# An attention loop on one core: shift by four reductions, token queries on two other engines, f32 products first in a group's last pair, all pair sums kept

## The chip, the cores and the metric

The kernel runs on one core of one Trainium2 chip. A core has TensorE (PE, matrix products, with weight loads shown as PEld), VectorE (DVE), ScalarE (ACT), GpSimd (POOL) and SyncE (SP), which issues most of the DMAs. The metric is the device time of the whole program in microseconds (us), lower is better. The kernel before takes 576.8 us (median of 3 runs, 575.64 to 578.02).

## The reference

Three layers stand behind each other: cross attention of 512 tokens (4 batches of 128, width 512) to 2048 context rows for each batch, a gated scan, and a mixture of 8 experts with two shared ones. The change touches the attention alone:

```
x = x + xattn(layernorm(x), ctx, ctx)
  q = x.reshape(B, T, 16, 32) * 32**-0.25          # 16 heads of 32
  k = ctx.reshape(B, S, 16, 32) * 32**-0.25; v = ctx.reshape(B, S, 16, 32)
  w = softmax(einsum('bthd,bshd->bhts', q, k))
  out = einsum('bhts,bshd->bthd', w, v).reshape(B, T, W) @ w_proj.T + b_proj
```

## The kernel before

The attention is cut into G = 16 groups: one batch and four heads (128 columns) each. A group needs, for each of its 4 heads, scores of 128 tokens against 2048 keys. Keys and queries are split into a high and a low float16 part, and three products (high x high, low x high, high x low) are stacked along the contraction, so KS = 96 rows give scores close to float32.

A group j passes through these steps, spread over the two groups before it:

- `split_keys(j, ...)`: ScalarE casts the float32 keys `kt` to `kh` (2 casts of 1024 elements to a partition), GpSimd subtracts to get `kl` (4 subtractions of 512, L587). SyncE's DMAs stack `kh`, `kl`, `kh` into `kstk`.
- `token_queries(j)` (L684, VectorE): two casts of the normed tokens into `xs` (L689, L690: the high part, twice) and one subtraction (L692: the low part). `queries(j)` (PE) transposes them and `take_queries` (ScalarE) copies them to `q1`.
- 16 times `max_scores(j, k)` (PE, L974: 512 keys of one head, into one of two PSUM banks) and `take_max` (VectorE, L697: the maximum along the 512). Product k waits until maximum k-2 has been taken, so PE and VectorE go in step with at most two between them.
- `shift(j)` (VectorE): the negated maximum of the four parts of a head (L701), its float16 high part (L704) and its low part (L706) go into two more columns of `xs`. `shifted(j)` (PE, L981) transposes the whole and `take_shifted` (ScalarE, L451) copies it to `q2`. So the maximum is subtracted within the score product.
- 8 times `scores(n)` (PE, L994: 2 tiles of 128 keys x 4 heads), `exponent(n)` (ScalarE, L462, 1024 elements), `values(n)` (PE, L1009, float32 products that weight `v`) and a denominator. The exponentials stand in a ring `pt` of 4. For 6 of the 8 numbers n of a group GpSimd adds the two tiles (`pair_sum`, L606) and PE multiplies the sum by ones (`denominators`, L1018: 4 float32 products); for the two in `PLAIN = (3, 7)` PE multiplies both tiles (`direct_denominators`, L1026: 8 products).
- `invert(i)` (L714) and `divide(i)` (L718) on VectorE, once all denominators of group i are there.

The order on each engine is written out by hand and is strict. PE's loop goes over pairs p = 0 to 3 of group i. In a pair it does, in this order, some maximum products of the next group (p = 3: of the one after), the two score products for numbers 8i+2p+2 and 8i+2p+3 with maximum products between them, the denominators of the pair before, `values` of 8i+2p and 8i+2p+1, and the direct denominators. In p = 1 `queries(i+2)` is put in; after p = 2 comes `shifted(i+1)`, and the scores of p = 3 are the first ones that need its `q2`. `MAXIMA` says how many maximum products stand in p = 0 to 3: 4, 4, 3, 5. ScalarE does in each pair the two exponentials, then `take_queries` (p = 1), a cast of the keys of group i+3 (p = 0, 1) or `take_shifted` (p = 2). GpSimd does the pair sums in order and, after numbers 3 and 5, two key subtractions each. VectorE takes the maxima of the pair, then `invert` and `divide` of the group before (p = 0), `shift(i+1)` (p = 2), `token_queries(i+3)` (p = 3). The last two groups have less beside them: no keys are split from group 13 on, and group 15 has no maxima of a next group.

SyncE loads keys three to four groups ahead and values one, and issues the constants and six weight tiles of the last layer during groups 13 and 14.

Of the kernel before, what the change touches and what calls it, by code (L numbers as in the profile page):

```python
# [83 lines left out]
def build_program(nc, t, out):  # L84
# [66 lines left out]
    mx = temp("mx", [P, HG, HG], F32)  # L151
    negm = temp("negm", [P, HG], F32)
    rden = temp("rden", [P, P], F32)
# [62 lines left out]
    win_done = sem("win_scaled")  # L216
    xs_step = sem("xs_step")
    qT_ready = sem("queries_transposed")
# [10 lines left out]
    den_done = sem("den_done")  # L229
    direct_done = sem("direct_denominators_done")  # L230
    o_rd = sem("o_reciprocal")
# [64 lines left out]

    PLAIN = (3, 7)
    SUMS = [hs for hs in range(HS) if hs not in PLAIN]
    NS, ND = len(SUMS), len(PLAIN)
    MAXIMA = (range(5, 9), range(9, 13), range(13, MB), range(0, 5))  # L300

    def sums(n):

        return NS * (n // HS) + len([hs for hs in SUMS if hs < n % HS])

    def plain(n):

        return n - sums(n)

    def is_plain(n):  # L310
        return n % HS in PLAIN

    def block_of(k):
        h, k = divmod(k, 2 * HG)
        return k // 2, 2 * h + k % 2

    def maxima_in(i, p):
# [106 lines left out]
    def _(act):  # L424
# [22 lines left out]
        def take_shifted(j):  # L447
            act.wait_ge(sh_ready, j + 1)
            if j >= 2:
                act.wait_ge(st_done, HS * (j - 1))  # L450
            act.activation(q2[:, j % 2, :, :], half_bank(6 + j % 2)[0:KM, 512:1024]  # L451
                           .rearrange("k (a t) -> k a t", a=HG), ACT.Copy).then_inc(q2_done, 1)

        def exponent(n):
            act.wait_ge(st_done, n + 1)
            if n >= 4:
                act.wait_ge(pv_done, n - 3)
                if is_plain(n - 4):
                    act.wait_ge(direct_done, plain(n - 3))
                else:  # L460
                    act.wait_ge(add_done, sums(n - 3))
# [6 lines left out]
        act.wait_ge(eps_set, 2)  # L468
        root(ln1_var, 1, 0, 1)
        for h in range(2):  # L470
            split_keys(1, h)
# [6 lines left out]
        exponent(0)  # L478
        exponent(1)
        for i in range(G):  # L480
# [102 lines left out]
    def _(pool):  # L583
# [10 lines left out]
        pool.memset(eps[:, 0:1], EPS).then_inc(eps_set, 1)  # L594
        pool.memset(eps[:, 1:2], EPS * 1e-8).then_inc(eps_set, 1)
        for a in range(2, HG):
            split_keys(0, a)
        for j in range(1, 3):
            for a in range(HG):
                split_keys(j, a)  # L600

        def pair_sum(n):
            pool.wait_ge(exp_done, n + 1)
            if sums(n) >= 4:
                pool.wait_ge(den_done, sums(n) - 3)
            pool.tensor_tensor(ps2[:, sums(n) % 4, :, :], pt[:, n % 4, 0, :, :], pt[:, n % 4, 1, :, :], ALU.add)\  # L606
                .then_inc(add_done, 1)
# [63 lines left out]
    def _(dve):  # L671
# [11 lines left out]

        def token_queries(j):  # L684
            q = xn[:, :, :].rearrange("p b (c n) -> p (b c) n", c=C)[:, j, :].rearrange("p (a d) -> p a d", a=HG)
            z = xs[:, j % 2, :, :]
            if j >= 2:
                dve.wait_ge(sh_ready, j - 1)
            dve.tensor_copy(z[:, :, 0:HD], q).then_inc(xs_step, 1)  # L689
            dve.tensor_copy(z[:, :, HD:2 * HD], q).then_inc(xs_step, 1)  # L690
            dve.wait_ge(xs_step, 3 * j + 1)
            dve.tensor_tensor(z[:, :, 2 * HD:KS], q, z[:, :, 0:HD], ALU.subtract).then_inc(xs_step, 1)  # L692

        def take_max(j, k):
# [4 lines left out]
        def shift(j):  # L699
            dve.wait_ge(m_taken, MB * (j + 1))  # L700
            dve.tensor_reduce(negm[:, :], mx[:, :, :], AX.X, ALU.max, negate=True).then_inc(mx_step, 1)  # L701
            dve.wait_ge(mx_step, 3 * j + 1)
            z = xs[:, j % 2, :, :]
            dve.tensor_copy(z[:, :, KS:KS + 1], negm[:, :].unsqueeze(2)).then_inc(mx_step, 1)  # L704
            dve.wait_ge(mx_step, 3 * j + 2)
            dve.tensor_tensor(z[:, :, KS + 1:KM], negm[:, :].unsqueeze(2), z[:, :, KS:KS + 1], ALU.subtract)\  # L706
                .then_inc(mx_step, 1)

        def invert(i):
            dve.wait_ge(den_done, NS * (i + 1))  # L710
            dve.wait_ge(direct_done, ND * (i + 1))
# [25 lines left out]
        dve.wait_ge(xn_done, 1)  # L737
        token_queries(0)
        token_queries(1)
        dve.wait_ge(x_in, 16)  # L740
# [4 lines left out]
        for j, k in maxima_in(-1, 3):  # L745
            take_max(j, k)
        token_queries(2)
        dve.wait_ge(roots, 2)
# [9 lines left out]
        for i in range(G):  # L758
            if i == G - 1:
                scale_win()  # L760
            for p in range(HS // 2):
# [5 lines left out]
                if p == 2 and i + 1 < G:  # L767
                    shift(i + 1)
                if p == 3 and i + 3 < G:
                    token_queries(i + 3)  # L770
        invert(G - 1)
# [184 lines left out]
    def _(pe):  # L956
        def queries(j):
            pe.wait_ge(xs_step, 3 * j + 3)
            if j >= 3:
# [17 lines left out]
        def shifted(j):  # L977
            pe.wait_ge(mx_step, 3 * j + 3)
# [35 lines left out]
        def denominators(n):  # L1014
            i, hs = divmod(n, HS)
            pe.wait_ge(add_done, sums(n) + 1)
            for a in range(HG):
                mm = pe.matmul(bank[a * HD:(a + 1) * HD, 6 + i % 2, P:2 * P], ones[:, :], ps2[:, sums(n) % 4, a, :],  # L1018
                               start=False, stop=(hs == SUMS[-1]), skip_group_check=True)
            mm.then_inc(den_done, 1)  # L1020

        def direct_denominators(n):
            i = n // HS
            for j in range(2):
                for a in range(HG):
                    mm = pe.matmul(bank[a * HD:(a + 1) * HD, 6 + i % 2, P:2 * P], ones[:, :], pt[:, n % 4, j, a, :],  # L1026
                                   start=False, stop=False, skip_group_check=True)
            mm.then_inc(direct_done, 1)

# [6 lines left out]
        shifted(0)  # L1036
        for i in range(-1, G):
            for p in range(HS // 2):
                if i < 0 and p < 3:
                    continue  # L1040
                tenants = maxima_in(i, p)
                for j, k in tenants[0:2]:
                    max_scores(j, k)
                for a, n in enumerate(scores_in(i, p)):
                    scores(n)
                    if p == 1 and a == 0 and i + 2 < G:
                        queries(i + 2)
                    for j, k in tenants[2 + a:3 + a]:
                        max_scores(j, k)
                for j, k in tenants[4:]:  # L1050
                    max_scores(j, k)
                if i < 0:
                    continue
                done = [HS * i + 2 * p, HS * i + 2 * p + 1]
                for n in (done[0] - 2, done[1] - 2):
                    if n >= 0 and not is_plain(n):
                        denominators(n)
                for n in done:
                    values(n)
                for n in done:  # L1060
                    if is_plain(n):
                        direct_denominators(n)
                if p == 2 and i + 1 < G:
                    shifted(i + 1)
        denominators(HS * (G - 1) + SUMS[-1])


# [241 lines left out]
```

## Time and profile before

| | us |
|---|---|
| median of 3 runs | 576.8 (575.64 to 578.02) |
| the profiled execution | 577.4 |
| its span, first to last instruction | 575.6 |
| PE busy | 484.5 (84%) |
| VectorE busy | 445.1 (77%) |
| ScalarE busy | 327.4 (57%) |
| GpSimd busy | 254.1 (44%) |

The attention fills the span's first 320 us or so. The profile is one execution; the busy shares are means over stages with different limits, so the stage of the attention is to be read by itself. The mean granted TensorE clock is 0.966 of full speed.

### The profile page before, as it was taken

How to read it: one execution, taken by the hardware profiler on the slowest of the kernel's cores; microseconds unless marked ns; L12 is line 12 of the kernel's file. 1: busy time of each engine (PE TensorE's matmuls, PEld its weight loads, DVE VectorE, ACT ScalarE, POOL GpSimd, SP SyncE). 2: the span in 40 equal slices, each digit the busy share in tenths (PEclk: the TensorE clock that was granted, in tenths of full speed). 3: DMA queues.
4: the chain of work that ended last, by engine and by line, in shares of the span. 5: the costliest groups of instructions: out<-in, count | busy, mean ns of one | idle time of the engine just before them, and what ended most of it. 6: DMA issues, size and time to landing. Idle time of an engine off the chain costs nothing.

```text
span 575.6 us, 16203 instructions
## 1 busy us (share of the span) xinstructions
PE 484.5 (84%) x6987; PEld 339.7 (59%) x6987; DVE 445.1 (77%) x635; ACT 327.4 (57%) x344; POOL 254.1 (44%) x230
## 2 busy tenths in 40 slices
PE   0468988889888898888998984879799999999993
PEld 0025666657666666665666561734488888887641
DVE  3576888888888888888872489888359999999416
ACT  3245655667556666557556253555349888888310
POOL 2356656777567676576546550456101110110050
PEclk9999989999899999899999996798899999999998
DMA  8696877677877778656599513239748999998143
GB/s 257 124 297 204 241 231 200 170 211 221 240 208 187 186 216 254 203 116 180 144 324 403 219 62 146 74 128 412 279 151 304 421 418 417 415 419 352 38 130 109
DMA packets 48252, 133.98 MB, mean 233 GB/s; under 512 B 6450, under 2 KB 31282, under 8 KB 37426
## 3 DMA queue, kind: packets, MB, share of 16 engines
q1 hardware_dynamic: 44500, 120.88, 64.7%
q0 software_dynamic: 3680, 12.06, 5.8%
q8 instruction: 55, 0.90, 0.6%
q14 instruction: 17, 0.14, 0.1%
HBM read 96.74 MB, written 11.01 MB: 187 GB/s over the span
## 4 chain that ended last, share of the span: by engine, by line
DVE 46%; PE 31%; issue 8%; DMA 8%; POOL 4%; ACT 2%; SPq 1%; DVEq 0%; ACTq 0%
DVE mx L697 17%; DVE ws L776 8%; PE bank L974 4%; PE bank L1009 4%; DMA kt<-in_keysT 4%; PE bank L994 3%; POOL xs_rows L651 3%; DVE xs L706 3%; PE bank L1018 3%; PE bank L1074 2%; DVE xs L690 2%; DVE rden L714 2%; DMA wst<-in_ffw 2%; DVE xs L704 2%; PE bank L1026 2%
## 5 line engine op out<-in xcount | busy, mean ns | idle before, releaser
L697 DVE TENSOR_REDUCE mx<-bank 128x1 f32<-128x512 f32 x256 | 163.3, 684 | 50.3 <-PE bank L974 49.2
L462 ACT ACTIVATE pt<-bank 128x1024 f32<-128x1024 f32 x128 | 128.2, 1023 | 81.7 <-PE bank L994 80.1
L606 POOL TENSOR_TENSOR ps<-pt 128x512 f32<-128x512 f32 x96 | 121.2, 1275 | 85.0 <-ACT pt L462 83.9
L776 DVE SCALAR_TENSOR_TENSOR ws<-wst,ws 128x2048 f16<-128x2048 f32 x51 | 116.5, 2301 | 2.3 <-ACT ws L501 2.1
L974 PE MATMUL bank<-kstk,q 96*128 96x512 f16 x256 | 95.0, 413 | 21.3 <-DVE mx L697 9.2
L501 ACT ACTIVATE ws<-wst 128x2048 f16<-128x2048 f32 x48 | 90.5, 1904 | 9.8 <-PE bank L1214 6.6
L587 POOL TENSOR_TENSOR kl<-kt,kh 128x512 f16<-128x512 f32 x62 | 70.5, 1160 | 40.3 <-ACT kh L432 40.3
L994 PEld LDWEIGHTS bank<-q,kstk 98*128 98x128 f16 x1024 | 69.0, 100 | 32.5 <-ACT q L451 12.9
L994 PE MATMUL bank<-q,kstk 98*128 98x128 f16 x1024 | 81.2, 225 | 5.5 <-ACT q L451 4.9
L1146 PE MATMUL bank<-xt,ws 128*128 128x128 f16 x480 | 81.2, 219 | 0.1
L1148 PE MATMUL bank<-xt,ws 128*128 128x128 f16 x480 | 81.2, 219 | 0.0
L1147 PE MATMUL bank<-xt,ws 128*128 128x128 f16 x480 | 81.2, 219 | 0.0
L1009 PE MATMUL bank<-pt,v 128*32 128x128 f32 x2048 | 69.6, 277 | 1.5 <-issue 1.5
L644 POOL DMA_DIRECT2D ys_rows<-xn x15 | 8.2, 543 | 120.3 <-ACT xn L568 120.3
L1009 PEld LDWEIGHTS bank<-pt,v 128*32 128x32 f32 x2048 | 58.8, 112 | 2.6 <-issue 2.3
L974 PEld LDWEIGHTS bank<-kstk,q 96*128 96x128 f16 x256 | 21.2, 100 | 50.4 <-DVE mx L697 33.1
L1146 PEld LDWEIGHTS bank<-xt,ws 128*128 128x128 f16 x480 | 47.0, 98 | 0.6 <-DVE hf L914 0.6
L432 ACT ACTIVATE kh<-kt 128x1024 f16<-128x1024 f32 x32 | 33.3, 1049 | 24.5 <-DMA kt<-in_keysT 24.5
L1148 PEld LDWEIGHTS bank<-xt,ws 128*128 128x128 f16 x480 | 47.0, 98 | 0.0
L1147 PEld LDWEIGHTS bank<-xt,ws 128*128 128x128 f16 x480 | 47.0, 98 | 0.0
L914 DVE SCALAR_TENSOR_TENSOR hf<-bank,win 128x512 f32<-128x512 f32 x23 | 15.8, 685 | 29.7 <-PE bank L1133 23.4
L1018 PE MATMUL bank<-ps,ones 128*32 128x128 f32 x768 | 35.7, 289 | 0.0
(163 smaller groups left out, 706.1 us busy)
## 6 DMA issues: line engine op xcount, KB each, us to landing
wst<-in_ffw SPq DMA_DIRECT2D x51, 1024.0 KB, 10.3
kt<-in_keysT SPq DMA_DIRECT2D x16, 1024.0 KB, 5.4
kstk<-kh SPq DMA_DIRECT2D x128, 128.0 KB, 3.1
v<-in_vals SPq DMA_DIRECT2D x16, 1024.0 KB, 6.5
kstk<-kl SPq DMA_DIRECT2D x64, 128.0 KB, 2.8
xs_rows<-biases SPq DMA_DIRECT2D x15, 256.0 KB, 3.1
x_tok<-xs_rows POOLq DMA_DIRECT2D x15, 256.0 KB, 8.6
ys_rows<-xn POOLq DMA_DIRECT2D x15, 256.0 KB, 6.9
```

What stands on the lines that cost most here:

```text
L462: act.activation(pt[:, n % 4, :, :, :].rearrange("p j a t -> p (j a t)"), bank[:, 2 * (n % 2):2 * (n % 2) + 2, :].rearrange("p j n -> p (j ...
L501: act.activation(ws[:, home_of(q), 0, m, :, :].rearrange("p c n -> p (c n)"), wst[:, q % 2, m, :, :].rearrange("p c n -> p (c n)"), ACT.Co ...
L587: low = pool.tensor_tensor(kl[:, j % 2, a, :], kt[:, j % 2, a, :], kh[:, j % 2, a, :], ALU.subtract)
L606: pool.tensor_tensor(ps2[:, sums(n) % 4, :, :], pt[:, n % 4, 0, :, :], pt[:, n % 4, 1, :, :], ALU.add)\
L697: dve.tensor_reduce(mx[:, a, q:q + 1], bank[:, 4 + k % 2, :], AX.X, ALU.max).then_inc(m_taken, 1)
L776: dve.scalar_tensor_tensor(ws[:, home_of(q), 1, m, :, :].rearrange("p c n -> p (c n)"), wst[:, q % 2, m, :, :].rearrange("p c n -> p (c n) ...
L974: pe.matmul(bank[:, 4 + k % 2, :], q1[:, j % 2, a, :], kstk[0:KS, j % 2, a, q * 512:(q + 1) * 512], start=True, stop=True).then_inc(m_read ...
L994: mm = pe.matmul(bank[:, 2 * (n % 2) + j, a * P:(a + 1) * P], kstk[:, i % 2, a, tile * P:(tile + 1) * P], q2[:, i % 2, a, :], start=True, ...
L1009: mm = pe.matmul(bank[a * HD:(a + 1) * HD, 6 + i % 2, 0:P], v[:, i % 2, tile, a * HD:(a + 1) * HD], pt[:, n % 4, j, a, :], start=(tile == ...
L1146: pe.matmul(o, ws[:, home, 0, m, c, part], xt[:, k % 2, c, :], start=(c == 0), stop=False)
L1147: pe.matmul(o, ws[:, home, 0, m, c, part], xt[:, k % 2, C + c, :], start=False, stop=False)
L1148: mm = pe.matmul(o, ws[:, home, 1, m, c, part], xt[:, k % 2, c, :], start=False, stop=(c == C - 1))
```

## The change

- `shift(j)` is four `tensor_reduce`: the negated maximum straight into the float16 column of `xs`; the same in float32 into `negm[..., 0]`; the float16 column negated into `negm[..., 1]`; the sum of the two into the second column. The casts and the subtraction are gone.
- `token_queries` is split: `queries_high` on ScalarE writes both high copies by one activation (read broadcast, 256 elements to a partition), `queries_low` on GpSimd subtracts. On ScalarE it stands after the two exponentials of p = 3, on GpSimd after the last pair sum of the group.
- PE's last pair (p = 3) does `shifted`, two maximum products, the denominators and values, and only then the scores with the other two maximum products. The other pairs stay.
- The maxima are 4, 5, 3, 4 for p = 0 to 3.
- `PLAIN` is gone: all 8 pair sums are made by GpSimd, and PE does 4 products for each.

```diff
-    PLAIN = (3, 7)
-    MAXIMA = (range(5, 9), range(9, 13), range(13, MB), range(0, 5))
+    MAXIMA = (range(4, 8), range(8, 13), range(13, MB), range(0, 4))
@@ scalar
+        def queries_high(j):
+            q, z = queries_of(j)
+            act.wait_ge(xn_done, j // C + 1)
+            if j >= 2:
+                act.wait_ge(sh_ready, j - 1)
+            act.activation(z[:, :, 0:2 * HD].rearrange("p a (r d) -> p a r d", r=2),
+                           q.unsqueeze(2).broadcast_to([P, HG, 2, HD]), ACT.Copy).then_inc(xs_hi, 1)
...
+                if p == 3 and i + 3 < G:
+                    queries_high(i + 3)
@@ gpsimd
+        def queries_low(j):
+            q, z = queries_of(j)
+            pool.wait_ge(xs_hi, j + 1)
+            pool.tensor_tensor(z[:, :, 2 * HD:KS], q, z[:, :, 0:HD], ALU.subtract).then_inc(xs_lo, 1)
...
-                if not is_plain(hs):
-                    pair_sum(HS * i + hs)
+                pair_sum(HS * i + hs)
...
+                if hs == HS - 1 and i + 3 < G:
+                    queries_low(i + 3)
@@ vector
-            dve.tensor_reduce(negm[:, :], mx[:, :, :], AX.X, ALU.max, negate=True).then_inc(mx_step, 1)
-            dve.tensor_copy(z[:, :, KS:KS + 1], negm[:, :].unsqueeze(2)).then_inc(mx_step, 1)
-            dve.tensor_tensor(z[:, :, KS + 1:KM], negm[:, :].unsqueeze(2), z[:, :, KS:KS + 1], ALU.subtract)
+            dve.tensor_reduce(z[:, :, KS:KS + 1], mx[:, :, :], AX.X, ALU.max, negate=True).then_inc(mx_step, 1)
+            dve.tensor_reduce(negm[:, :, 0:1], mx[:, :, :], AX.X, ALU.max, negate=True).then_inc(mx_step, 1)
+            dve.wait_ge(mx_step, 4 * j + 1)
+            dve.tensor_reduce(negm[:, :, 1:2], z[:, :, KS:KS + 1], AX.X, ALU.max, negate=True).then_inc(mx_step, 1)
+            dve.wait_ge(mx_step, 4 * j + 3)
+            dve.tensor_reduce(z[:, :, KS + 1:KM], negm[:, :, :], AX.X, ALU.add).then_inc(mx_step, 1)
@@ tensor
+            if i + 1 < G:
+                shifted(i + 1)
+            tenants = maxima_in(i, 3)
+            for j, k in tenants[0:2]:
+                max_scores(j, k)
+            second_products(i, 3)
+            for a, n in enumerate(scores_in(i, 3)):
+                scores(n)
+                for j, k in tenants[2 + a:3 + a]:
+                    max_scores(j, k)
```

## Rows read from the trace of the kernel before

**Rows 1.** The page: busy us of each engine, share of the span, instructions.
```profile
PE 484.5 (84%) x6987; PEld 339.7 (59%) x6987; DVE 445.1 (77%) x635; ACT 327.4 (57%) x344; POOL 254.1 (44%) x230
```

**Rows 2.** Windows: start:end us, length, busy us (instructions) by engine, clock, DMA.
```profile
48.60:65.40 16.80, 15.01 (x300) 10.92 (x297) 14.01 (x23) 10.30 (x12) 11.94 (x10) 1.00 0.71 196
65.40:279.15 213.75, 186.01 (x3556) 134.33 (x3552) 181.34 (x289) 131.62 (x144) 144.01 (x120) 0.98 0.73 200
279.15:295.55 16.40, 15.15 (x300) 10.95 (x297) 12.56 (x22) 9.03 (x10) 7.50 (x6) 1.00 0.73 200
295.55:309.83 14.28, 12.59 (x287) 9.95 (x283) 8.12 (x17) 8.13 (x9) 6.83 (x7) 1.00 1.02 398
309.83:319.47 9.64, 7.55 (x212) 6.54 (x209) 0.52 (x2) 5.54 (x6) 7.51 (x7) 1.00 0.67 276
```

**Rows 3.** Timeline of one steady group: start us, us, engine, line, [idle before <-releaser].
```profile
125.73 0.17 DVE L701 TENSOR_REDUCE negm<-mx 128x4 f32<-128x16 f32 x1
...
128.08 0.42 PE L981 MATMUL bank<-idh,xs 128*98 128x128 f16 x4 [1.46 <-DVE xs L706]
...
128.55 0.60 ACT L451 ACTIVATE q<-bank 98x512 f16<-98x512 f16 x1 [2.09 <-PE bank L981]
```

**Rows 4.** Waits in 65.4 to 279.15 us: us in total, times, longest.
```profile
PE bank L981 <- DVE xs L706: 17.5, 12, 1.5
```

**Rows 5.** Instructions of single VectorE lines: duration ns min/median/max.
```profile
L701 DVE TENSOR_REDUCE negm<-mx x16: 169/170/170, 33.0 to 302.2; 128x4 f32<-128x16 f32 x16
L704 DVE CAST xs<-negm x16: 178/876/955, 33.2 to 302.4; 128x4 f16<-128x4 f32 x16
L706 DVE TENSOR_TENSOR xs<-negm,xs x16: 177/1185/1189, 33.4 to 303.4; 128x4 f16<-128x4 f32 x16
L690 DVE CAST xs<-xn x16: 212/1307/1318, 12.5 to 274.8; 128x128 f16<-128x128 f32 x16
L692 DVE TENSOR_TENSOR xs<-xn,xs x16: 276/278/285, 12.7 to 276.0; 128x128 f16<-128x128 f32 x16
```

**Rows 6.** Timeline of group 13, which has no key splits and no token queries.
```profile
281.55 0.64 PE L1018 MATMUL bank<-ps,ones 128*32 128x128 f32 x16
...
282.01 1.06 PE L1009 MATMUL bank<-pt,v 128*32 128x128 f32 x32
...
282.89 0.62 PE L1026 MATMUL bank<-pt,ones 128*32 128x128 f32 x16
...
283.44 0.61 PE L974 MATMUL bank<-kstk,q 96*128 96x512 f16 x2
...
287.21 0.42 PE L981 MATMUL bank<-idh,xs 128*98 128x128 f16 x4 [0.52 <-DVE xs L706]
...
288.32 0.62 PE L994 MATMUL bank<-q,kstk 98*128 98x128 f16 x8 [0.26 <-ACT q L451]
```

**Rows 7.** The page's costliest groups: count, busy us, mean ns, idle before.
```profile
L697 DVE TENSOR_REDUCE mx<-bank 128x1 f32<-128x512 f32 x256 | 163.3, 684 | 50.3 <-PE bank L974 49.2
L462 ACT ACTIVATE pt<-bank 128x1024 f32<-128x1024 f32 x128 | 128.2, 1023 | 81.7 <-PE bank L994 80.1
L606 POOL TENSOR_TENSOR ps<-pt 128x512 f32<-128x512 f32 x96 | 121.2, 1275 | 85.0 <-ACT pt L462 83.9
...
L587 POOL TENSOR_TENSOR kl<-kt,kh 128x512 f16<-128x512 f32 x62 | 70.5, 1160 | 40.3 <-ACT kh L432 40.3
```

**Rows 8.** Windows of two neighbouring groups: the second with the lower clock.
```profile
128.00:145.50 17.50, 15.14 (x296) 10.94 (x296) 15.09 (x25) 10.98 (x12) 11.97 (x10) 1.00 0.77 212
145.50:164.20 18.70, 16.57 (x296) 11.97 (x296) 15.12 (x25) 11.03 (x12) 12.03 (x11) 0.91 0.72 198
```

**Rows 9.** Timeline of the start: the token queries of group 2 and what follows.
```profile
39.81 0.40 DVE L689 CAST xs<-xn 128x128 f16<-128x128 f32 x1
...
41.55 0.16 DVE L726 RECIPROCAL lnv<-lnv 128x3 f32<-128x3 f32 x1
...
44.94 0.61 PE L974 MATMUL bank<-kstk,q 96*128 96x512 f16 x1 [3.53 <-DVE mx L697]
```

More of the change, by code:

```diff
@@ L216, in build_program @@
     win_done = sem("win_scaled")
-    xs_step = sem("xs_step")
+    xs_hi = sem("queries_high")
+    xs_lo = sem("queries_low")
     qT_ready = sem("queries_transposed")
@@ L457, in exponent @@
                 act.wait_ge(pv_done, n - 3)
[L458 to L461, printed above, removed]
+                act.wait_ge(add_done, n - 3)
             act.activation(pt[:, n % 4, :, :, :].rearrange("p j a t -> p (j a t)"),
@@ L469, in _ @@
         root(ln1_var, 1, 0, 1)
+        queries_high(0)
+        queries_high(1)
         for h in range(2):
@@ L479, in _ @@
         exponent(1)
+        queries_high(2)
         for i in range(G):
@@ L600, in _ @@
                 split_keys(j, a)
+        queries_low(2)
         def pair_sum(n):
             pool.wait_ge(exp_done, n + 1)
-            if sums(n) >= 4:
-                pool.wait_ge(den_done, sums(n) - 3)
-            pool.tensor_tensor(ps2[:, sums(n) % 4, :, :], pt[:, n % 4, 0, :, :], pt[:, n % 4, 1, :, :], ALU.add)\
+            if n >= 4:
+                pool.wait_ge(den_done, n - 3)
+            pool.tensor_tensor(ps2[:, n % 4, :, :], pt[:, n % 4, 0, :, :], pt[:, n % 4, 1, :, :], ALU.add)\
                 .then_inc(add_done, 1)
@@ L700, in shift @@
             dve.wait_ge(m_taken, MB * (j + 1))
[L701 to L702 removed]
             z = xs[:, j % 2, :, :]
[L704 to L707 removed]
+            dve.tensor_reduce(z[:, :, KS:KS + 1], mx[:, :, :], AX.X, ALU.max, negate=True).then_inc(mx_step, 1)
[3 more added lines that the diff above has]
+            dve.wait_ge(mx_step, 4 * j + 3)
+            with nc.allow_low_precision(reason="the sum of two terms is exact and rounded once"):
+                dve.tensor_reduce(z[:, :, KS + 1:KM], negm[:, :, :], AX.X, ALU.add).then_inc(mx_step, 1)
         def invert(i):
[L710 to L711 removed]
+            dve.wait_ge(den_done, HS * (i + 1))
             if i > 0:
@@ L957, in queries @@
         def queries(j):
[L958 removed]
+            pe.wait_ge(xs_lo, j + 1)
             if j >= 3:
@@ L1015, in denominators @@
             i, hs = divmod(n, HS)
-            pe.wait_ge(add_done, sums(n) + 1)
+            pe.wait_ge(add_done, n + 1)
             for a in range(HG):
-                mm = pe.matmul(bank[a * HD:(a + 1) * HD, 6 + i % 2, P:2 * P], ones[:, :], ps2[:, sums(n) % 4, a, :],
-                               start=False, stop=(hs == SUMS[-1]), skip_group_check=True)
+                mm = pe.matmul(bank[a * HD:(a + 1) * HD, 6 + i % 2, P:2 * P], ones[:, :], ps2[:, n % 4, a, :],
+                               start=False, stop=(hs == HS - 1), skip_group_check=True)
             mm.then_inc(den_done, 1)
[L1022 to L1028, printed above, removed]
         pe.wait_ge(ones_set, 1)
@@ L1036, in _ @@
         shifted(0)
[L1037 to L1042, printed above, removed]
-                    max_scores(j, k)
[L1044 to L1050, printed above, removed]
-                    max_scores(j, k)
[L1052 to L1064, printed above, removed]
@@ L1065, in _, with first_products @@
-        denominators(HS * (G - 1) + SUMS[-1])
+        def first_products(i, p):
+            tenants = maxima_in(i, p)
+            for j, k in tenants[0:2]:
+                max_scores(j, k)
+            for a, n in enumerate(scores_in(i, p)):
+                scores(n)
+                if p == 1 and a == 0 and i + 2 < G:
+                    queries(i + 2)
+                for j, k in tenants[2 + a:3 + a]:
+                    max_scores(j, k)
+            for j, k in tenants[4:]:
+                max_scores(j, k)
@@ new lines, in second_products @@
+        def second_products(i, p):
+            done = [HS * i + 2 * p, HS * i + 2 * p + 1]
+            for n in (done[0] - 2, done[1] - 2):
+                if n >= 0:
+                    denominators(n)
+            for n in done:
+                values(n)
+        first_products(-1, 3)
+        for i in range(G):
+            for p in range(3):
+                first_products(i, p)
+                second_products(i, p)
+            if i + 1 < G:
+                shifted(i + 1)
+            tenants = maxima_in(i, 3)
+            for j, k in tenants[0:2]:
+                max_scores(j, k)
+            second_products(i, 3)
+            for a, n in enumerate(scores_in(i, 3)):
+                scores(n)
+                for j, k in tenants[2 + a:3 + a]:
+                    max_scores(j, k)
@@ L1068, in _ @@
+        denominators(HS * G - 2)
+        denominators(HS * G - 1)
         pe.wait_ge(consts, NC)
```

32 lines of the change are left out of this document (7 added, 25 removed).

## The prediction

> **What bounds the kernel now.** I read the busy times first. Over the whole span TensorE has 84% and VectorE 77% [rows 1], but that mixes three layers, and the change lies in one. So I cut the attention at the moments at which PE begins p = 1 of a group [rows 2]: 16.80 us for the first group, 213.75 for the next twelve (17.81 each), 16.40 for group 13, then 14.28 and 9.64. In an undisturbed steady group of 17.50 us PE is busy 15.14, VectorE 15.09, ScalarE 10.98, GpSimd 11.97 [rows 8]. No engine is full. PE and VectorE take turns.
>
> The timeline shows where they do not overlap. PE reaches `shifted` and stands still for 1.46 us while VectorE does the three instructions of the shift, then waits again for ScalarE's copy [rows 3]. In the twelve steady groups that first wait is 17.5 us in twelve places [rows 4]. The reason is seen in the durations: the reduction at L701 takes 170 ns always, but the cast of 4 elements 876 ns in the median and 178 at best, the subtraction of 4 elements 1185 against 177, and the second query cast 1307 against 212 [rows 5]. The small values occur where GpSimd is idle. So these three lines wait for GpSimd's running instruction, and the reduction doesn't. A steady group thus has a VectorE that loses some 3 us to waiting that is recorded as busy.
>
> **The change, part by part.**
>
> *Shift.* Out: 876 + 1185 ns. In: three reductions more, 170 ns each [rows 5]. The new ones read 4 to 16 elements as L701 does, and I take its price; a float16 output is not shown, so from 0.17 up to the 0.88 of the cast for each float16 one. VectorE: -2.06 + 0.51 = -1.55 us. The mx-to-PE path falls from 2.3 us to some 0.8, so the 1.46 us wait at L981 goes to nothing: what PE has before it (values of p = 2, 0.88 us by the spacing of [rows 6]) then covers the shift.
>
> *Token queries.* VectorE loses 0.37 + 1.31 + 0.28 = 1.96 us less what it overlaps, say 1.7. Together VectorE goes from 15.1 to 11.9 us for a group. That is no longer a bound. The work reappears elsewhere. ScalarE's activation of 256 elements: a quarter of the 1.02 for 1024 [rows 7] is 0.26, the 0.60 for 512 [rows 3] is the upper end; I take 0.35. ScalarE goes to 11.3 us of 15 and hides it. GpSimd's subtraction of 128 elements: a quarter of 1.16 is 0.29, the whole 1.16 the upper end [rows 7]; I take 0.35, near the proportional one.
>
> The Trainium skill (GPSIMD Engine Reference, Engine selection) puts elementwise work with two inputs at about twice VectorE's time on GpSimd. On the 278 ns of L692 [rows 5] that would be an estimated 0.56 us, 0.2 more for a group than my value, and on a GpSimd that then bounds 13 groups some 2.7 us more in all, 545 in place of 542. No row here shows so small a GpSimd subtraction.
>
> *All pair sums.* Out: two direct blocks on PE of 283.44 - 282.89 = 0.55 us each. In: two more denominators of 0.23 us, half of the 282.01 - 281.55 = 0.46 that a pair takes [rows 6]. PE: -0.64 us. GpSimd: two more pair sums, +2.55. Its group is now 8 x 1.275 + 4 x 1.16 + 0.35 = 15.2 us by mean durations, or 11.97 + 2.55 + 0.35 = 14.9 by busy time [rows 7, 8]. This is the part that costs: an engine with 5.5 us of air gets none.
>
> *f32 first in p = 3.* `shifted`, two maximum products, denominators and values now fill the 0.7 us in which ScalarE copies `q2`; the 0.26 us wait of the first scores [rows 6] goes. The price is that exponentials 8 and 9 start some 1.4 us later in the pair (denominators 0.46, values 0.88) and that `queries_high` stands behind them, then `queries_low`, and behind that on GpSimd all pair sums of the next group. I followed this loop: queries_low 0.35, six pair sums 7.65, two key subtractions 2.32, then PE's denominators, values and one score block 0.46 + 0.88 + 0.62, two exponentials 2.05 and queries_high 0.35, sum 14.7 us. It is below 15, but with under 1 us of slack.
>
> *Maxima 4, 5, 3, 4* only move one product from p = 3 to p = 1. I take nothing for it: it costs a wait of about 0.2 for the fifth maximum in p = 1, and gives it back in p = 3. If VectorE were still late, it would be 0.68 [rows 7].
>
> *Transfers.* The DMA share of 0.73 to 0.77 at 17.5 us [rows 2, 8] becomes 0.88 at 15. Loads stand a group ahead or more, so they stay hidden; the narrowest is the stack of the group after next. In group 14 the share is already 1.02 [rows 2]; there I give no more than 1 us.
>
> *The new group.* PE's path: 17.50 - 1.46 - 0.26 - 0.64 = 15.1 us. The same from group 13: 16.40 - 0.52 - 0.26 - 0.64 = 15.0. GpSimd: 14.9 to 15.2. Two chains of equal length that hand over to each other seldom both run full; I add 0.15 to the larger and take 15.35 us.
>
> The clock. Three of the twelve steady groups are like the second of [rows 8], 1.2 us longer at a mean granted clock of 0.91 against 1.00; 12 x 17.5 + 3 x 1.2 = 213.6 gives the whole 213.75. Just before it fell PE stood in the same 1.46 us wait. With that wait gone I expect fewer such groups and keep one.
>
> *The start.* VectorE does token queries of group 2 from 39.81 to 41.55, and PE waits 3.53 us for the next maximum until 44.94 [rows 9]; without them it comes 1.7 us earlier. The first pair sums come about 1 us later on GpSimd, not on the path. The queries of groups 0 and 1 end while ScalarE waits for keys: 0.
>
> *The end.* The last denominator now waits for a pair sum of 1.28 us after the last exponential; PE has values left beside it and saves the direct block. I take 0, between -0.5 and +1.
>
> *Sum,* against the profiled execution (577.4, span 575.6): start -1.7; group 0: 16.80 to 15.35, -1.45; twelve groups: 213.75 to 12 x 15.35 + 1.2 = 185.4, -28.35; group 13, without key splits: 16.40 to 15.05, -1.35; group 14: its wait at the shift 0.5, the q2 wait and one direct block 0.3, -1.1; group 15: 0. In all -33.95. What follows the attention starts earlier and is unchanged. 577.4 - 34 = 543.4 for the profiled execution; the median is 0.6 below it, so **542.8 us**.
>
> **Rivals.**
>
> *A: GpSimd binds harder.* The subtraction costs near 1.1 us, or the handoff (ScalarE's queries_high behind exponential 9, queries_low behind that) leaves it idle about 1 us a group. For it: both chains have under 1 us of slack. Against: VectorE's casts, the other side of the conflict, are gone. The group is 16.2 us: 13 x 0.85 = 11 more, 554.
>
> *B: everything overlaps.* GpSimd's instructions follow each other closer than their durations (busy 11.97 against a sum of 12.3, [rows 7, 8]), no group has the lower clock, and the group is 14.9: 13 x 0.45 + 1.2 = 7 less, 536.
>
> *C: slower.* One mechanism, in GpSimd's queue: it is full, and everything waits for it (exponentials through the ring of 4, denominators, queries), so whatever its instructions lose goes straight into the time. The gain of 34 us over 13 groups is 2.6 each, so it decides from a group of 15.35 + 2.6 = 18.0 us. A pair sum would then take (18.0 - 4.64 - 0.35) / 8 = 1.63 us in place of 1.275, as it would if it lost 0.35 to each of VectorE's maxima beside it. At 18.4 the time is 577 + 5 = 582. Against it: L606 has 1275 ns in the mean [rows 7] with such maxima beside it already.
>
> *D: the gain does not arrive.* The reductions to float16 columns wait for GpSimd as the casts do (two of four at 0.9 to 1.2 us), VectorE keeps some 2 us of shift and PE a wait of about 1.2. Then the group is 16.5, 558. That L701 never waited speaks against it, and the output type is all that differs.
>
> **From the cases to the numbers.** The forecast has 0.58, A 0.2, B 0.14, C 0.03, D 0.05. The range 536 to 556 holds the forecast, B to its centre and A to a little above its own. About 0.5% (2.9 us) is what a measurement of this kernel can tell from no change. Only C is slower; faster 0.95, same 0.02 for a gain that is lost behind the attention, slower 0.03.
>
> **What would show it.** The four reductions at 0.17 us and no idle time before L981's successor; the interval between two `invert` at 15.2 to 15.5 us; GpSimd busy 97% or more of a steady group, PE about the same; ScalarE's new line at 0.35 and GpSimd's at 0.3 to 0.4 us; no more than one or two stretches of lower clock up to the end of the attention; the attention's end near 286 in place of 320. Wrong would be the sum if GpSimd shows idle time released by ScalarE before queries_low in each group, if PE waits for pair sums at the denominators, or if a maximum waits for PE as long as now though the shift is short.

## The result, and the profile after

The changed kernel takes 547.85 us (median of 4 runs, 544.2 to 555.9) against 577.4 for the kernel before (4 runs): ratio 0.9487, 95% interval 0.943 to 0.9544. A second series gave 547.25 against 576.74, ratio 0.9471, interval 0.9412 to 0.953. The first ratio goes by four fast runs (544.2, 547.45, 548.24 and 550.06 us) and leaves out the slow one of 555.9. Forecast were 542.8 (536 to 556). The profiled execution is the fastest of its series: 544.2 us, span 542.4; its forecast was 543.4.

The busy times of the page answer to [rows 1]: VectorE has 45 us less, PE 12 less, GpSimd 44.5 more.

```profile
PE 472.5 (87%) x6731; PEld 329.3 (61%) x6731; DVE 399.8 (74%) x603; ACT 330.3 (61%) x360; POOL 298.6 (55%) x278
```

The next view cuts the attention after the change at the reciprocals of VectorE (one for each group): start:end, length, then busy us of PE, PEld, VectorE, ScalarE, GpSimd, clock, DMA share, GB/s. It answers to [rows 2, 8].

```profile
139.06:155.38 16.32, 14.70 (x292) 10.50 (x284) 11.79 (x24) 11.15 (x14) 14.74 (x14) 1.00 0.92 256
155.38:170.56 15.18, 14.52 (x292) 10.44 (x284) 11.78 (x23) 11.13 (x14) 14.73 (x14) 1.00 0.86 232
...
233.68:248.86 15.18, 14.52 (x292) 10.44 (x284) 11.78 (x23) 11.13 (x14) 14.72 (x14) 1.00 0.68 166
248.86:264.05 15.19, 14.54 (x292) 10.46 (x284) 11.79 (x23) 8.95 (x11) 11.27 (x10) 1.00 0.68 166
264.05:278.06 14.01, 12.64 (x280) 9.61 (x272) 9.13 (x20) 8.29 (x10) 9.59 (x8) 1.00 1.03 399
278.06:286.38 8.32, 7.80 (x225) 6.69 (x214) 1.25 (x3) 5.68 (x6) 8.32 (x8) 1.00 1.01 417
```

Two things are to be seen. A steady group that nothing disturbs takes 15.18 or 15.19 us, each time, where it took 17.53. And there is a second kind, seven of the twelve, 0.5 to 1.2 us longer, at a full granted clock in this profile. The row of 248.86 is group 13, without key splits: GpSimd is busy 3.5 us less, and the group is as long. So GpSimd, though busy 97% of the other quiet groups, is not what bounds them.

The new and rewritten lines, durations in ns as min/median/max, answer to [rows 5]:

```profile
L701 DVE TENSOR_REDUCE xs<-mx x16: 176/178/180, 32.2 to 271.3; 128x4 f16<-128x16 f32 x16
L702 DVE TENSOR_REDUCE negm<-mx x16: 157/158/160, 32.3 to 271.4; 128x4 f32<-128x16 f32 x16
L704 DVE TENSOR_REDUCE negm<-xs x16: 158/160/163, 32.4 to 271.5; 128x4 f32<-128x4 f16 x16
L707 DVE TENSOR_REDUCE xs<-negm x16: 173/175/176, 32.6 to 271.7; 128x4 f16<-128x8 f32 x16
L449 ACT ACTIVATE xs<-xn x16: 399/418/419, 12.1 to 246.7; 128x256 f16<-128x256 f32 x16
L599 POOL TENSOR_TENSOR xs<-xn,xs x16: 417/420/653, 12.6 to 247.2; 128x128 f16<-128x128 f32 x16
```

No reduction waits, with GpSimd running beside it almost always. The shift is 0.58 us from its first start to its last end, and the timeline of a quiet group, which answers to [rows 3], has it over before PE comes to its transposes:

```profile
162.62 0.18 DVE L701 TENSOR_REDUCE xs<-mx 128x4 f16<-128x16 f32 x1
...
163.03 0.17 DVE L707 TENSOR_REDUCE xs<-negm 128x4 f16<-128x8 f32 x1
...
163.67 0.42 PE L975 MATMUL bank<-idh,xs 128*98 128x128 f16 x4
```

Where the time went, by the starts of the reciprocals. What stands behind the last one took 256.0 us before and after.

| stretch | before | after | forecast |
|---|---|---|---|
| up to the first reciprocal | 64.89 | 60.19 | -3.15 |
| twelve steady groups | 213.75 | 188.67 | -28.35 |
| group 13 | 16.40 | 15.19 | -1.35 |
| the next interval | 14.06 | 14.01 | -1.1 |
| the last interval | 10.50 | 8.32 | 0 |
| sum | 319.60 | 286.38 | -33.95 |

188.67 is 12 x 15.18 = 182.2 and 6.5 us of long groups. One of them, in the timeline (SPq is SyncE's issuing of DMAs):

```profile
135.52 0.60 SPq L327 DMA_DIRECT2D kt<-in_keysT  x1
136.16 0.44 SPq L332 DMA_DIRECT2D v<-in_vals  x1
...
138.28 2.63 SPq L337 DMA_DIRECT2D kstk<-kh  x4
...
140.95 2.75 SPq L337 DMA_DIRECT2D kstk<-kl  x2
...
147.35 0.42 PE L975 MATMUL bank<-idh,xs 128*98 128x128 f16 x4
...
148.75 0.59 PE L968 MATMUL bank<-kstk,q 96*128 96x512 f16 x2 [0.97 <-issue]
```

PE idles 0.97 us in front of the first maximum product of the last pair and no engine is named as its releaser ("issue"). Each of the seven long groups has one such wait, of 0.31 to 1.00 us, and is longer than a quiet one by that wait and 0.1 to 0.2 us; no quiet group has one. In 60 to 265 us (total, times, longest):

```profile
PE bank L968 <- issue: 5.3, 7, 1.0
```

That product needs the first half of the stack of group i+2, six DMAs that stand in the queues behind 2 MB of keys and values issued 2 us earlier. This was my guess for the long groups, and the first thing to test. The rival was the clock, which had made the long groups before [rows 8].

### The profile page after: what moved, and what is told of

It reads as the page before. It is cut to its first block, busy times and chain, and to the rows that moved or that the text cites. A ratio compares the mean times of both kernels' runs of the same rounds, so it can differ in the third digit from the quotient of the medians.

```text
span 542.4 us, 15769 instructions
## 1 busy us (share of the span) xinstructions
PE 472.5 (87%) x6731; PEld 329.3 (61%) x6731; DVE 399.8 (74%) x603; ACT 330.3 (61%) x360; POOL 298.6 (55%) x278
## 4 chain that ended last, share of the span: by engine, by line
PE 43%; DVE 33%; DMA 8%; issue 7%; POOL 5%; ACT 2%; SPq 1%; DVEq 0%; ACTq 0%; POOLq 0%
DVE mx L696 11%; DVE ws L770 9%; PE bank L1003 8%; PE bank L968 8%; PE bank L1012 7%; PE bank L988 6%; DMA kt<-in_keysT 4%; POOL xs_rows L660 3%; DMA wst<-in_ffw 3%; DVE rden L713 2%; PE bank L1126 2%; PE bank L1127 2%; PE bank L1128 2%; DVE hf L908 1%; DMA xs_rows<-ao_wproj,posu 1%
## 5 line engine op out<-in xcount | busy, mean ns | idle before, releaser
L696 DVE TENSOR_REDUCE mx<-bank 128x1 f32<-128x512 f32 x256 | 163.1, 686 | 66.1 <-PE bank L968 65.4
L614 POOL TENSOR_TENSOR ps<-pt 128x512 f32<-128x512 f32 x128 | 160.0, 1279 | 10.8 <-PE bank L1012 5.6
L457 ACT ACTIVATE pt<-bank 128x1024 f32<-128x1024 f32 x128 | 125.8, 1023 | 65.9 <-PE bank L988 65.8
L968 PE MATMUL bank<-kstk,q 96*128 96x512 f16 x256 | 96.4, 407 | 24.9 <-DVE mx L696 7.8
L988 PE MATMUL bank<-q,kstk 98*128 98x128 f16 x1024 | 80.0, 222 | 1.3 <-ACT pt L457 1.0
L1012 PE MATMUL bank<-ps,ones 128*32 128x128 f32 x1024 | 41.4, 279 | 0.0
## 6 DMA issues: line engine op xcount, KB each, us to landing
xs_rows<-biases SPq DMA_DIRECT2D x15, 256.0 KB, 3.0
x_tok<-xs_rows POOLq DMA_DIRECT2D x15, 256.0 KB, 8.6
ys_rows<-xn POOLq DMA_DIRECT2D x15, 256.0 KB, 6.5
```

The source lines that it names most:

```text
L614: pool.tensor_tensor(ps2[:, n % 4, :, :], pt[:, n % 4, 0, :, :], pt[:, n % 4, 1, :, :], ALU.add)\
L696: dve.tensor_reduce(mx[:, a, q:q + 1], bank[:, 4 + k % 2, :], AX.X, ALU.max).then_inc(m_taken, 1)
L968: pe.matmul(bank[:, 4 + k % 2, :], q1[:, j % 2, a, :], kstk[0:KS, j % 2, a, q * 512:(q + 1) * 512], start=True, stop=True).then_inc(m_read ...
L988: mm = pe.matmul(bank[:, 2 * (n % 2) + j, a * P:(a + 1) * P], kstk[:, i % 2, a, tile * P:(tile + 1) * P], q2[:, i % 2, a, :], start=True, ...
```

## The experiments

The intervals between reciprocals in one profile of each kernel, worked out from the starts, are the measure of a group. The granted clock is 1.00 unless given:

| kernel | median us | quiet group | long groups in the profile |
|---|---|---|---|
| before | 577.4 | 17.53 | 3 of 18.6 (clock 0.91) |
| changed, first series | 547.85 | 15.19 | 7 of 15.7 to 16.4 |
| e1 changed again | 547.25 | 15.19 | 7 of 15.8 to 17.4 |
| e2 stack first | 543.11 | 15.19 | 4 of 15.4 to 16.3, one 19.3 (clock 0.91) |
| e3 values once | 537.92 | 15.19 | none |
| e4 before, stack first | 577.37 | 17.0 to 17.8 | 2, 18.5 and 19.0 (clock 0.91) |
| e5 loads spread | 538.77 | 15.19 | 2, 16.0 and 16.6 |
| e6 old shift | 570.03 | 16.46 | 2, 21.7 and 22.5 (clock 0.92, 0.85) |
| e7 old queries | 594.61 | 17.7 (clock 0.98) | 8 of 20.1 to 20.3 (clock 0.84), two behind each of 17.7 |
| e8 old sums | 554.17 | 15.84 | 4 of 16.2 to 18.3 |
| e9 scores first | 547.94 | 15.17 | 3 of 16.0 to 16.9, 3 of 18.2 to 18.6 (clock 0.91) |
| e10 before, new shift | 554.63 | 16.01 | 2, 17.5 and 16.6 |
| e11 spread, third maximum | 538.14 | 15.19 | none |
| e12 the same, maxima 4, 4, 4, 4 | 535.66 | 14.90 | 1 of 15.6 |

e1 to e4, e5 to e8 and e9 to e12 were measured on three chips, where the kernel before took 576.74, 576.47 and 577.67 us; the ratios are each against the same chip. The start varies from profile to profile: with one order of loads the first reciprocal comes at 61.89 (e5), 61.47 (e11) and 60.10 us (e12). So medians 1 or 2 us apart are not told apart by four runs.

### e1 to e4: what makes a group long

**e1**, the changed kernel again.

> The changed kernel once more, as the yardstick of this chip. Theory (late stack): seven of the sixteen groups in the first profile are 0.5 to 1.2 us longer than 15.19 because the first maximum product of the last pair waits for its stacked keys; which groups these are differs from run to run, so the time is between 544 and 550 us, and groups without that wait take 15.19 us again. Rival (clock): the long groups are those with a lower granted clock; then they show under 1.00.

547.25 us; quiet groups of 15.19 and seven long ones, not the same as in the first profile. As expected. Each has the wait in front of the same product again, of 0.40 to 2.05 us, at a clock of 1.00.

**e2**, SyncE's order:

```diff
+            if i + 2 < G:
+                stack(i + 2, 0)
             if i + 4 < G:
                 load_k(i + 4)
             if i + 1 < G:
                 load_v(i + 1)
             if i + 2 < G:
-                stack(i + 2, 0)
                 stack(i + 2, 1)
```

> Only SyncE's order is changed: the first half of the key stack of group i+2 is issued ahead of the load of keys i+4 and of values i+1. Theory (late stack): the 2 MB of keys and values no longer stand before the stack, no wait of 0.5 to 1.1 us is left in front of the first maximum product of the last pair, all steady groups take 15.2 us, and the time is 6 us under e1 (about 538), with less spread. Rival (clock, or instruction fetch): the same time as e1 within 1 us. Rival (lateness only moves to the loads of keys and values): as e1 or slower, with waits on those loads.

543.11 us, ratio 0.9417 (0.9354 to 0.9481): 4 us in the medians, not clear of e1 by the intervals, and not the 538 expected. The waits in 60 to 265 us (total, times, longest) show why, and name the transfer:

```profile
ACT kh L423 <- DMA kstk<-kl: 7.3, 6, 3.3
...
PE bank L969 <- DMA kstk<-kl: 4.4, 5, 2.2
```

They sit in p = 1 now: the second half of the stack is late, since the 2 MB stand before that one. The third expectation came nearest, only that the wait was not on the moved loads but on what now follows them. The group of 19.3 us has the longest of these waits and something more:

```profile
203.05 1.03 PE L969 MATMUL bank<-kstk,q 96*128 96x512 f16 x2 [2.15 <-DMA kstk<-kl]
```

Behind it, from 203 to 207 us, the mean granted clock is 0.58, and PE is busy 16.20 us in the group where a quiet one has 14.53. So part of this group's length is the clock.

**e3**, no values in the queue (groups from 2 on use old ones):

```diff
-            if i + 1 < G:
+            if i == 0:
                 load_v(i + 1)
...
-                pe.wait_ge(v_in[i % 2], 16 * (i // 2 + 1))
+                pe.wait_ge(v_in[i % 2], 16)
```

> Values are loaded for groups 0 and 1 alone and used again by all later groups (the output is then not the reference's); 14 MB of transfers are left out of the attention, SyncE's order is as in the changed kernel. Theory (late stack): the wait before the last pair goes here too, groups of 15.2 us, about 538 us. If the time is bound by PE and VectorE and not by transfers, it is not lower than e2. Rival (transfers slow the whole loop): groups below 15.2 us, under 536.

537.92 us, and every steady group takes 15.19 or 15.20. Two of them:

```profile
93.58:108.78 15.20, 14.54 (x292) 10.46 (x284) 11.80 (x23) 11.15 (x14) 14.73 (x14) 1.00 0.75 206
108.78:123.97 15.19, 14.53 (x292) 10.45 (x284) 11.79 (x23) 11.13 (x14) 14.72 (x14) 1.00 0.62 141
```

So the transfers make the long groups: with the values' megabyte of each group left out they are gone, while the quiet group is as long as in e1, to 0.01 us. The rival that transfers slow the whole loop is out.

**e4**, e2's order in the kernel before.

> The kernel before with e2's order of SyncE. Its groups of 17.5 us leave 2.3 us more for the transfers, and no wait for a stack is seen in its trace. Theory: no change, 577 within 1 us. Rival (the order helps by itself, in both kernels): 2 us or more faster.

577.37 us, ratio 1.0008 (0.998 to 1.0036). The trace of the kernel before has no wait of PE for a stack, so there is none to take away. The new order even brings two such waits of PE (60 to 265 us: 1.1 us together), and the median does not show them. In e10, at 16.0 us a group, PE has four waits of that kind with the old order, up to 1.66 us. The lateness came with the speed.

### e5: the transfers spread

```diff
             if i + 4 < G:
                 load_k(i + 4)
             if i + 2 < G:
                 stack(i + 2, 0)
+            if i + 1 < G:
+                load_v(i + 1)
+            if i + 2 < G:
                 stack(i + 2, 1)
```

(and without the `load_v` between the first two.)

> SyncE's order once more: keys i+4, first half of the stack i+2, then values i+1, then the second half; so no megabyte stands directly behind another, and each half of the stack has one of them ahead of it and not two. e2 only moved the two behind the first half, and its waits went to the second half (up to 2.2 us at the first maximum product of p = 1). Theory (transfers pile up in two places of a group, not their sum): nearly all steady groups at 15.2 us, time at the level of e3, 538 to 541, 6 us under e1. Rival (at 15.2 us a group the transfers are too many in sum, share 0.83 and up): waits remain wherever the loads stand, 543 to 547.

538.77 us, ratio 0.9334 (0.9294 to 0.9374), below e1's interval. Eleven of the thirteen steady intervals are quiet; in 60 to 260 us PE's waits for a stack are down to two:

```profile
PE bank L969 <- DMA kstk<-kl: 0.9, 1, 0.9
PE bank L969 <- issue: 0.7, 1, 0.7
```

All bytes are moved, as in e1; only where they stand has changed. It was a pile-up of the transfers, and not their sum, that made most of the waits.

### e6 to e9: one part undone at a time

**e6**, the shift with the cast and subtraction of before, in the changed kernel.

```diff
-            dve.tensor_reduce(z[:, :, KS:KS + 1], mx[:, :, :], AX.X, ALU.max, negate=True)
...
+            dve.tensor_reduce(negm[:, :], mx[:, :, :], AX.X, ALU.max, negate=True)
+            dve.tensor_copy(z[:, :, KS:KS + 1], negm[:, :].unsqueeze(2))
+            dve.tensor_tensor(z[:, :, KS + 1:KM], negm[:, :].unsqueeze(2), z[:, :, KS:KS + 1], ALU.subtract)
```

> The changed kernel with the old shift (reduction, cast, subtraction on VectorE), all else changed. Theory: the cast and the subtraction each wait for GpSimd's running instruction, which is now nearly always there, so 0.9 to 1.3 us each; the shift takes 2.3 us in place of 0.68, values of p = 2 hide some 0.5 of it, PE waits 1.1 us at the transposes, the group is 16.3 us and the time about 560. Rival (the shift was no part of it, VectorE had room enough): within 2 us of e1.

570.03 us, 14 to 32 us above e1: the four runs (560.98, 569.24, 570.82, 578.95) lie too far apart for a ratio, and the profiled one took 569.24. The expected 560 is at their lower end. The quiet group is 16.46 us, 1.27 longer, near the 1.1 expected. What I had not expected are two groups of some 22 us. The timeline of the first:

```profile
67.42 2.52 POOL L614 TENSOR_TENSOR ps<-pt 128x512 f32<-128x512 f32 x2
...
69.01 5.62 DVE L703 CAST xs<-negm 128x4 f16<-128x4 f32 x1
69.89 2.27 POOL L587 TENSOR_TENSOR kl<-kt,kh 128x512 f16<-128x512 f32 x2
72.11 2.48 POOL L614 TENSOR_TENSOR ps<-pt 128x512 f32<-128x512 f32 x2
74.66 0.18 DVE L705 TENSOR_TENSOR xs<-negm,xs 128x4 f16<-128x4 f32 x1
...
74.89 0.66 PE L974 MATMUL bank<-idh,xs 128*98 128x128 f16 x4 [4.97 <-DVE xs L705]
```

A cast of 4 elements lasts 5.62 us: it starts while GpSimd's second sum runs, four more GpSimd instructions follow without a gap, and it ends with the last of them. PE stands 4.97 us. The other long group shows the same 5.62 us. In a quiet group of this profile (from 83.22 us) the cast starts as far into the same sum, GpSimd's next instruction follows as closely, and the cast lasts 0.94 us, to the end of the sum that was running. What decides between the two is not in the trace. Part of the two groups' length is again the clock (0.92 and 0.85, PE busy 1.4 and 2.3 us more than in a quiet group).

**e7**, the token queries on VectorE again, behind the maxima of p = 3: the two casts and the subtraction of before, `queries_high` and `queries_low` gone.

> The changed kernel with the token queries on VectorE again (two casts, one subtraction, behind the maxima of p = 3). Theory: with GpSimd nearly always busy each of the two casts waits, some 2.5 to 3 us in a stretch in which VectorE has no idle time (from the third maximum of p = 3 to the reciprocal); the group grows by 2 us or more to 17.3, 575. Rival (PE's path of 15.1 us bounds, VectorE has 3 us of idle time): 16.0 us a group or less, under 557.

594.61 us, ratio 1.0296 (1.0232 to 1.036): slower than the kernel before. The theory had the direction and 28 of the 47 us over e1. The casts, now two in a row, take these ns:

```profile
L688 DVE CAST xs<-xn x16: 216/956/1002, 13.3 to 292.6; 128x128 f16<-128x128 f32 x16
L689 DVE CAST xs<-xn x16: 215/1298/1299, 13.4 to 293.4; 128x128 f16<-128x128 f32 x16
```

That is 2.3 us in a stretch in which PE needs VectorE:

```profile
121.51 0.39 PE L973 MATMUL bank<-kstk,q 96*128 96x512 f16 x1 [2.06 <-DVE mx L696]
```

By that the group should be some 17.3 us. One in three is near it, at 17.7; the windows of three neighbours show what the others have besides:

```profile
105.62:123.31 17.69, 14.98 (x288) 10.73 (x284) 14.20 (x25) 10.37 (x12) 14.26 (x13) 0.98 0.70 197
123.31:143.40 20.09, 17.40 (x288) 12.21 (x284) 14.44 (x25) 11.42 (x14) 14.53 (x13) 0.84 0.69 196
143.40:163.66 20.26, 17.57 (x288) 12.31 (x284) 14.45 (x25) 10.88 (x13) 14.39 (x13) 0.84 0.65 184
```

At a mean granted clock of 0.84 PE is busy 2.4 to 2.6 us more with the same 288 matmuls, and the group is longer by just that. VectorE's and GpSimd's work is the same. So the wait goes with 2.5 us (17.69 against 15.19, of which PE's wait above accounts for 2.06), and the lower clock with about the same again, in two groups of three.

**e8**, two direct denominators again.

```diff
+    PLAIN = (3, 7)
...
-                pair_sum(HS * i + hs)
+                if not is_plain(hs):
+                    pair_sum(HS * i + hs)
```

> The changed kernel with two direct denominators in a group again. GpSimd is relieved by 2.55 us, PE does 0.64 us more. Theory (PE and VectorE bound the group, GpSimd does not, as the 15.19 us of group 13 without key splits show): slower by up to 0.6 us a group, 15.6 to 15.8, 552 to 556. Rival (GpSimd bounds the group): faster than e1.

554.17 us, ratio 0.963 (0.9584 to 0.9677), 7 us above e1. The quiet group is 15.84, 0.65 longer: PE's 0.64 us, worked out from [rows 6], arrives whole. Relieving GpSimd brings nothing. So work on PE lengthens the group one for one, and GpSimd does not bound it. PE's path is more than its own work, though: PE is busy 14.5 of the 15.19 us, and e12 finds 0.29 us of it in waits for VectorE.

**e9**, scores ahead of the float32 products in the last pair:

```diff
+            for p in range(4):
+                first_products(i, p)
+                second_products(i, p)
+                if p == 2 and i + 1 < G:
+                    shifted(i + 1)
```

> The changed kernel with the scores ahead of the float32 products in the last pair again, maxima 4, 5, 3, 4 as changed. Theory: PE then waits for ScalarE's copy of q2, 0.3 to 0.7 us a group, and nothing else moves: 15.5 to 15.9 us a group, 551 to 556. Rival (the order only decides who waits, and earlier exponentials give it back, as the 1.5 us that ScalarE idles there in the changed kernel suggest): 15.2 or less, as e1.

547.94 us, ratio 0.9478 (0.9435 to 0.9521), as e1. The rival had it: the quiet group is 15.17 us, 0.02 shorter, although in the quiet groups PE does wait again for ScalarE's copy:

```profile
119.88 0.62 PE L988 MATMUL bank<-q,kstk 98*128 98x128 f16 x8 [0.26 <-ACT q L441]
```

So this part of the change is worth nothing on its own, in quiet groups and in the median. The long groups differ: three of the six have a clock of 0.91 and PE busy 16.3 us, behind waits for the stack of 1.41, 1.76 and 1.63 us. A wait of 1.73 us in this profile and one of 2.05 in e1 left the clock at 1.00, so the length of the wait alone does not decide it, and one profile of each does not show that the order does. What takes the 0.26 us back was not found: the string of maxima on VectorE, my candidate, falls with e11. e12 points to another, the wait for the fifth maximum of p = 1, which was not tested with this order.

### e10: the shift alone

The four reductions in the kernel before, nothing else.

> The kernel before with the four reductions alone. Theory: the wait of 1.46 us at the transposes goes, 17.53 to 16.1 us in twelve steady groups, -17 us, and the groups of lower clock go with it, -3: 556 to 559. Rival (the shift gives less alone, since VectorE still makes the queries with casts that wait, and that bounds the group): 565 or more.

554.63 us, ratio 0.9634 (0.9569 to 0.9699): 3.7% of the changed kernel's 5.3%. The quiet group is 16.01 us, as expected; no group has a lower clock, and the two long ones (17.53 and 16.61 us) have waits for the stack:

```profile
PE bank L975 <- issue: 2.8, 4, 1.7
```

In the timeline PE's transposes wait for nothing, while the query cast on the same VectorE waits as ever:

```profile
102.90 0.17 DVE L708 TENSOR_REDUCE xs<-negm 128x4 f16<-128x8 f32 x1
...
103.32 0.42 PE L982 MATMUL bank<-idh,xs 128*98 128x128 f16 x4
...
107.47 1.32 DVE L690 CAST xs<-xn 128x128 f16<-128x128 f32 x1
```

The two kernels e10 and e7 differ only in the sums, the order of the last pair and the maxima; both leave the queries on VectorE. With all the sums on GpSimd that is 594.61 us, with six of eight 554.63. e8 has the queries moved too, the new order and maxima, and six of eight sums on GpSimd, and takes 554.17, with a quiet group of 15.84. So moving the queries earned next to nothing there, and is what lets GpSimd take the last two sums.

### e11 and e12: can it be faster

**e11**: e5 with the third maximum product of p = 3 between denominators and values.

```diff
-            second_products(i, 3)
+            denominators(HS * i + 4)
+            denominators(HS * i + 5)
+            for j, k in tenants[2:3]:
+                max_scores(j, k)
+            values(HS * i + 6)
+            values(HS * i + 7)
```

> e5 with the third maximum product of p = 3 between the denominators and the values, and not behind the first scores. In the changed kernel VectorE idles about 1.1 us twice there, and then has no idle time until the reciprocal, while PE waits 0.45 and 0.28 us for maxima in p = 0. Theory (a string of maxima on VectorE from p = 3 to the division is part of the 15.19 us): 0.4 to 0.7 us less a group, 14.6 to 14.8, 530 to 533. Rival (PE's own work bounds): 15.1 to 15.2, as e5.

538.14 us, ratio 0.9316 (0.9272 to 0.9359), quiet groups 15.19: the theory fell. The third maximum product comes earlier, between denominators and values, and the group does not move.

**e12**: e11 with maxima 4, 4, 4, 4.

```diff
-    MAXIMA = (range(4, 8), range(8, 13), range(13, MB), range(0, 4))
+    MAXIMA = (range(4, 8), range(8, 12), range(12, MB), range(0, 4))
```

> e11 with maxima 4, 4, 4, 4: the fifth of p = 1 goes to p = 2. Theory: PE's wait of 0.4 us for the fifth goes, but the shift ends 0.63 us later, of which the values of p = 2 hide 0.45: 0 to 0.3 us less a group than e11, 528 to 533. Rival (the shift comes on the path again): 0.2 us more a group, 535.

535.66 us, ratio 0.9292 (0.9241 to 0.9344). The quiet group is 14.90 us, 0.29 shorter, and the waits of the maxima's weight loads for VectorE (60 to 260 us) fall from the first line, e11's, to the second, one fewer in each group, that for the fifth maximum of p = 1:

```profile
PEld bank L969 <- DVE mx L697: 19.2, 52, 0.5
...
PEld bank L969 <- DVE mx L697: 13.4, 40, 0.5
```

The later shift is still covered: PE's transposes do not wait for it, only their weight loads do, by 0.2 us. The theory of up to 0.3 us less a group held, its 528 to 533 us did not, since it counted on a gain of e11 that did not come. e12 is the fastest kernel of the study, 12 us under the changed one by the medians of two series; its interval lies below that of e1, but overlaps those of e5 and e11.

## Why the prediction was right, step by step

*What bounds before.* VectorE's casts and subtraction waiting for GpSimd was read rightly from min and median of the same line. e6, e7 and e10 show it from three sides. The 64 reductions of the shift took 157 to 180 ns beside a GpSimd busy 97% of a quiet group. By the Trainium skill (SBUF — State Buffer, Who interferes with whom) a cast can contend with GpSimd, an operation with two inputs in SBUF contends with GpSimd's reads, and on trn2 a reduction never contends; the traces agree.

*Shift.* Forecast 0.17 each, measured 0.16 to 0.18. The wait of 1.46 us at the transposes is gone; values of p = 2 cover it, as said.

*Queries.* ScalarE 0.42 (0.35 taken), GpSimd 0.42 (0.35 taken). In a quiet group GpSimd idles 0.5 us for ScalarE's half. The prediction named that as a sign against its sum; the sum held all the same, since GpSimd does not bound the group. The Trainium skill's factor of two (GPSIMD Engine Reference, Engine selection) had given an estimate of 0.56 us, which was on the high side of the 0.42 measured.

*Pair sums.* GpSimd busy 14.73 us, forecast 14.9. That it would bind (rival A) fell with group 13 and e8; the sum had taken GpSimd's 15.2 us as the larger of the two chains. PE's saving of 0.64 us was right: undoing it costs 0.65 (e8).

*f32 first.* Priced at the removal of 0.26 us. e9: nothing. That term was wrong.

*The steady group.* PE's path was worked out as 15.1 and measured as 15.18. The 0.15 us added for friction was not needed. That the path came out so well is in part luck: it holds the 0.26 us that e9 found to be nothing. The parts that were measured are the shift, 17.53 to 16.01 us (e10), and the sums, 0.65 (e8); they leave 15.36, and the remaining 0.17 us, of queries, maxima and order together, was not taken apart. Group 13 was worked out as 15.0, taken as 15.05 without a reason, and measured as 15.19.

*Transfers.* "They stay hidden" is the step that failed. The share went to 0.86 and 0.92 as foreseen (0.88), but I had only asked whether a load is issued a group ahead, not what stands before it in the queues. It costs 6.5 us in the profile, and by e1 against e5, 547.25 to 538.77, some 8.5 in the median. The forecast had the clock in its place, 1.2 us. The clock's long groups were gone, and gone in e10 too, where only the shift is changed; the new ones had another cause. The argument from the wait in front of them is not shown by that: in e6 the quiet groups have a wait of 1.19 us at the transposes and a clock of 1.00. With the waits nearly gone (e5) the median is 4 us under the forecast, with them 5 above it: too much friction and too little queueing had partly made up for each other.

*Start and end.* Up to the first reciprocal -4.7 against -3.15; the difference of 1.5 us is within the 1.8 by which the start varies (e5, e12). VectorE's normalisation of batches 1 to 3 starts at 38.07 in place of 41.55 us. Of these 3.5 us, 1.7 are the query casts as forecast, and 0.8 were there before the first shift (32.19 against 33.00 us); the rest was not taken apart. The next-to-last interval gave 0.05 where 1.1 was forecast, the last 2.2 where 0 was: together -2.2 against -1.1.

## What to carry to other kernels

Where a tiny VectorE instruction has a median far over its minimum, look at what GpSimd does beside it, and replace the cast or the two-input form by a reduction or give it to ScalarE, before loading GpSimd further: the added GpSimd work that costs nothing in quiet groups makes the old queries cost 47 us (e7, some 20 of them through the clock). The old shift costs 23 us in the kernel before (577.67 against e10's 554.63) and 14 to 32 in the changed one (e6). When a loop gets faster, check each transfer's landing against its use again, by what is queued ahead of it and not by how early it is issued; one megabyte in each gap instead of two in one was worth 8.5 us (e5), as much as the pair sums (7 us, e8). A part worked out as a gain may be covered by the next wait: undo it alone to know.

## What the runs showed of the hardware that was not expected

A VectorE cast of 128x4 lasted 5.6 us, twice in one profile (e6), and each time ended with the last of several GpSimd instructions that followed each other without a gap, while in other groups of the same profile it ended with the one that was running (median 949 ns), though the next followed as closely. So such a wait can be longer than GpSimd's running instruction; what decides it stays open.

Quiet groups have the same length to 0.01 us with a DMA share of 0.68 or of 0.86 beside them: up to the point at which something waits for a landing, the engines did not feel the traffic.

A wait for a late transfer can cost twice: in e2 and e9 the granted clock fell to a mean of 0.58 and 0.50 in stretches of 3 to 4 us behind such waits, and PE was busy 1.7 or 1.8 us more in the group. In e1 no group shows it, with waits up to 2.05 us.
